# Turning the first chunk of two passes earlier, halving the last chunk, and moving a branch, in a four-layer graph kernel

## The reference, cut to what matters

```python
x = _layernorm(x + _L0_gnn_ref(x, adj, L0_gnn_embedding, L0_gnn_weight, L0_gnn_bias))
x = _layernorm(x + _L1_gnn_ref(x, 0, L1_gnn_net_params, adj))        # z = relu((adj @ z) @ w[i]), twice
x = _layernorm(x + _L2_gnn_ref(x, adj, w_self, w_neighbor, bias))    # x @ w_self + (adj @ x) @ w_neighbor + bias
x = _layernorm(x + _L3_gnn_ref(x, adj, adj, weight, bias))           # [x, A x, 2AAx-x, A x, 2AAx-x] @ weight + bias
```

## Time and profile before

| what | us |
|---|---|
| median of 3 runs | 1255.47 (1253.18 to 1255.48) |
| the profiled execution, whole | 1256.36 |
| its span, first to last instruction | 1254.4 |
| PE busy in the span | 1230.7 (98%) |
| DVE busy | 758.2 (60%) |
| ACT, POOL busy | 215.7, 62.7 |

### The profile page before, as it was taken

How to read it: one execution, slowest core, us unless ns; L and a number is a source line. 1 busy time by engine, 2 the same in 40 slices (tenths; PEclk the granted TensorE clock), 3 DMA queues, 4 the chain that set the end, 5 groups by cost and what they waited for, 6 DMA issues and landing times.

```text
span 1254.4 us, 16358 instructions
## 1 busy us (share of the span) xinstructions
PE 1230.7 (98%) x5872; PEld 1031.1 (82%) x5872; DVE 758.2 (60%) x1863; ACT 215.7 (17%) x392; POOL 62.7 (5%) x52
## 2 busy tenths in 40 slices
PE   8999999999999999999999999999999999999996
PEld 6888888888888887888888888878888888888875
DVE  5825898777777877788725554552246255545624
ACT  6622111120111101120111111110111111111110
POOL 0000000000000000000000001010000000010100
PEclk9999999999999999999999999999999999999998
DMA  9832112111111110101011133043011111320320
GB/s 343 328 101 60 32 45 76 56 57 38 58 55 55 47 38 28 40 22 42 15 34 35 32 79 71 5 118 67 1 37 31 35 34 30 85 65 7 95 58 36
DMA packets 128646, 78.16 MB, mean 62 GB/s; under 512 B 97312, under 2 KB 108064, under 8 KB 126752
## 3 DMA queue, kind: packets, MB, share of 16 engines
q1 hardware_dynamic: 128560, 77.05, 21.2%
HBM read 53.42 MB, written 23.59 MB: 61 GB/s over the span
## 4 chain that ended last, share of the span: by engine, by line
PE 93%; DVE 3%; DMA 2%; SPq 1%; issue 1%; ACT 0%; DVEq 0%
PE ps L679 29%; PE ps L680 29%; PE ps L783 22%; PE ps L697 8%; PE ps L718 2%; PE ps L719 2%; DMA raw<-in_at 1%; PE ps L691 1%; DVE nat L1045 1%; DVE ring L1045 1%; DMA td<-ring 0%; DMA ring<-td 0%; SPq L1087 0%; DVE ring L931 0%; DVE sml L987 0%
## 5 line engine op out<-in xcount | busy, mean ns | idle before, releaser
L679 PE MATMUL ps<-B,xs 128*128 128x512 f32 x1664 | 655.0, 394 | 1.5 <-DVE xs L943 1.5
L680 PE MATMUL ps<-B,xs 128*128 128x512 f32 x1664 | 648.2, 390 | 0.0
L679 PEld LDWEIGHTS ps<-B,xs 128*128 128x128 f32 x1664 | 312.9, 188 | 64.2 <-issue 1.6
L680 PEld LDWEIGHTS ps<-B,xs 128*128 128x128 f32 x1664 | 312.9, 188 | 62.5
L783 PE MATMUL ps<-Tw,xs 128*128 128x512 f32 x1280 | 309.4, 391 | 0.9 <-DVE ring L1045 0.9
L783 PEld LDWEIGHTS ps<-Tw,xs 128*128 128x128 f32 x1280 | 238.4, 188 | 53.3 <-DVE ring L1045 4.2
L931 DVE TENSOR_TENSOR ring<-ps,rrep 128x512 f32<-128x512 f32 x94 | 64.5, 689 | 259.1 <-PE ps L680 247.5
L1045 DVE SCALAR_TENSOR_TENSOR nat<-ps,embn,nat 128x128 f32<-128x128 f32 x448 | 153.3, 342 | 51.5 <-PE ps L783 51.3
L1045 DVE SCALAR_TENSOR_TENSOR ring<-ps,embn,ring 128x128 f32<-128x128 f32 x512 | 174.8, 341 | 0.0
L697 PEld LDWEIGHTS ps<-W,ring 128*128 128x128 f32 x896 | 112.7, 193 | 10.7 <-issue 3.1
L697 PE MATMUL ps<-W,ring 128*128 128x128 f32 x896 | 114.3, 277 | 3.4 <-DMA ring<-td 2.3
(11 more groups left out here) (66 smaller groups left out, 569.2 us busy)
## 6 DMA issues: line engine op xcount, KB each, us to landing
raw<-in_at SPq DMA_DIRECT2D x13, 1024.0 KB, 16.9
td<-ring SPq DMA_DIRECT2D x32, 256.0 KB, 2.1
ring<-td SPq DMA_DIRECT2D x128, 64.0 KB, 2.5
ring<-in_xn SPq DMA_DIRECT2D x16, 256.0 KB, 2.9
ring_x<-in_xt SPq DMA_DIRECT2D x32, 128.0 KB, 3.2
ring_x<-y1d SPq DMA_DIRECT2D x32, 128.0 KB, 3.2
out<-nat SPq DMA_DIRECT2D x16, 256.0 KB, 2.3
y1d<-ring SPq DMA_DIRECT2D x14, 256.0 KB, 2.8
```

The costliest lines, as they stand in the source:

```text
L679: pe.matmul(bank, x[:, 0, m, :], of, start=m == 0, stop=False)
L680: mm = pe.matmul(bank, x[:, 1, m, :], of, start=False, stop=ends and m == NT - 1)
```

## The change

It has three parts.

1. The step `turn` of the first chunk of passes 4 and 5 stands where the lane's previous pass ends (behind its last `normed`), ahead of the first of the two hand-overs, and its `back` stands behind that hand-over. Both stood at the first chunk's own product. The second chunk's `turn` and `back` move up by two quarters of the first chunk's product.
2. In the very last pass (pair 1, pass 6) the last chunk of 512 columns is done as two of 256, numbered 4 and 5, with a hand-written order. The last multiplication of `normed` for chunks 1 and 2 of that pass goes from DVE to POOL (`pooled`), and chunks are written out as they become ready. Chunk 5's `centre` waits for POOL's `normed` of chunk 1, whose small buffer it reuses.
3. DVE, ACT, POOL and SP read the flag behind the step `scale` of chunk 1 of that pass (`CUT`), a chunk and a half before the end. The general body stands in the branch that is taken if the flag is set, and the remaining steps of the fast one behind it, in the `Else`. PE still reads the flag at its end.

The diff, cut to its core:

```diff
-            if p == 6 and j != 1:
+            if p == 6:
                 put("out", j, 6, c)
+        if (j, p) == (1, 6):
+            order = order[:12]
         for c, m in order:
-            if p in (4, 5) and (c, m) == (0, 0):
-                turn(0, 0)
-            if p in (4, 5) and (c, m) == (0, 1):
-                put("back", j, p, 0, 0)
-            if p in (4, 5) and c < 3 and m == 2:
+            if p in (4, 5) and c < 3 and m == (2 if c else 0):
                 turn(c + 1, 0)
-            if p in (4, 5) and c < 3 and m == 3:
+            if p in (4, 5) and c < 3 and m == (3 if c else 1):
                 put("back", j, p, c + 1, 0)
...
+        if (j, p) == (1, 6):
+            for m in range(4):
+                put("mm", j, p, 4, m)
+                if m == 1:
+                    put("after", j, p, 2)
+                    put("deviate", j, p, 1)
+                    put("centre", j, p, 2)
+            put("scale", j, p, 4)
+            put("normed", j, p, 1)
+            exchange(1)
+            put("mm", j, p, 5, 0)
+            put("mm", j, p, 5, 1)
+            put("deviate", j, p, 2)
+            put("normed", j, p, 2)
+            exchange(2)
+            put("after", j, p, 4)
+            put("centre", j, p, 4)
+            put("mm", j, p, 5, 2)
+            put("mm", j, p, 5, 3)
+            put("scale", j, p, 5)
+            put("deviate", j, p, 4)
+            put("after", j, p, 5)
+            put("centre", j, p, 5)
+            put("normed", j, p, 4)
+            exchange(4)
+            put("deviate", j, p, 5)
+            put("normed", j, p, 5)
+            exchange(5)
+            return
...
         for p in (4, 5, 6):
+            if p < 6:
+                put("turn", j, p, 0, 0)
             yield
+            if p < 6:
+                put("back", j, p, 0, 0)
...
-END = STEPS.index(Step("out", 1, 6))
+CUT = STEPS.index(Step("scale", 1, 6, 1)) + 1
+
+def pooled(s):
+    return (s.j, s.p) == (1, 6) and s.c in (1, 2)
...
+                        if c == 4:
+                            dv.wait_ge(s_norm, norm_at[Step("normed", j, p, 0)])
+                        if c == 5:
+                            dv.wait_ge(s_pn, pool_at[Step("normed", j, p, 1)])
...
+                    if s.kind == "normed" and pooled(s):
+                        po.wait_ge(s_rec, rec_at[s])
+                        po.tensor_tensor(g, g, sml[:, n, c, 0, :].unsqueeze(2).to_broadcast([P, 8, C]),
+                                         ALU.mult).then_inc(s_pn, 1)
...
-                fast.dve(eng, STEPS)
+                fast.dve(eng, STEPS[:CUT])
                 eng.wait_ge(s_flag, 1)
                 v = eng.value_load(flag[0:1, 0:1], min_val=0, max_val=N)
                 with eng.If(v != 0):
...
                     slow.dve(eng, STEPS)
+                with eng.Else():
+                    fast.dve(eng, STEPS[CUT:])
...
-                fast.sp(eng, STEPS[:END])
+                fast.sp(eng, STEPS[:CUT])
...
-                with eng.If(v == 0):
-                    fast.sp(eng, STEPS[END:])
-                with eng.Else():
+                with eng.If(v != 0):
                     fast.sp_start(eng)
                     slow.sp_start(eng)
                     slow.sp(eng, STEPS)
+                with eng.Else():
+                    fast.sp(eng, STEPS[CUT:])
```

More of the change, by code:

```diff
@@ L23 @@
 LAST = 15
+SPAN = [(512 * c, 512) for c in range(NC)] + [(1536, 256), (1792, 256)]
 PIECES = {0: 4, 1: 2, LAST: 4}
@@ L275, in second @@
                     yield
-        if j == 1:
-            for c in range(NC):
-                put("out", j, 6, c)
     def whole_pair(j):
@@ L470, in way @@
             prep2_at = {s: 2 * v for s, v in numbered("prep2").items()}
-            mean_at, var_at, norm_at = numbered("centre"), numbered("deviate"), numbered("normed")
+            mean_at, var_at, rec_at = numbered("centre"), numbered("deviate"), numbered("normed")
+            norm_at = {s: i + 1 for i, s in enumerate(s for s in rec_at if not pooled(s))}
+            pool_at = {s: i + 1 for i, s in enumerate(s for s in rec_at if pooled(s))}
             n_T = len(T_at)
@@ L581, in way @@
                         sq_after[s] = held_q[n]
-                        held_q[n] = (s_var, var_at[Step("deviate", s.j, s.p, s.c)])
+                        if s.c != 4:
+                            held_q[n] = (s_var, var_at[Step("deviate", s.j, s.p, s.c)])
             def tile_landed(m, c):
@@ L591, in piece, with span, within @@
                 return slice(c * width, (c + 1) * width)
+            def span(c):
+                return slice(SPAN[c][0], sum(SPAN[c]))
+            def within(slot, c):
+                return slot[:, 256 * (c - 4):256 * (c - 3)] if c > 3 else slot
             def ch(t, c):
-                return t[:, c * 512:(c + 1) * 512]
+                return t[:, span(c)]
             def groups(t, c):
@@ L618, in y_slot @@
                             ring[:, 4, :], ring[:, 5, :], ring_x[:, 0, :], ring_x[:, 1, :]][4 * j + c]
-                return ring[:, 4 + j % 2, :]
+                return within(ring[:, 4 + j % 2, :], c)
             def square_slot(j, p, c):
@@ L625, in square_slot @@
                     return rrep[:, 1536:2048] if general else ring_g[:]
-                return ps[:, 6 + j % 2, :]
+                return within(ps[:, 6 + j % 2, :], c)
             def part_slot(c):
@@ L677, in pe_quarter @@
                 for m in range(4 * k, 4 * k + 4):
-                    of = B[:, m, c * 512:(c + 1) * 512]
+                    of = B[:, m, span(c)]
                     pe.matmul(bank, x[:, 0, m, :], of, start=m == 0, stop=False)
@@ L681, in pe_quarter, with pe_rest @@
                 return mm
-            def pe_rest(pe, x, bank, v):
+            def pe_rest(pe, x, bank, c, v):
                 for m in range(NT):
                     pe.wait_ge(s_glo, 16 * (v - 1) + m + 1)
-                    pe.matmul(bank, x[:, 0, m, :], glo[:], start=False, stop=m == NT - 1).then_inc(s_gmm, 1)
+                    pe.matmul(bank, x[:, 0, m, :], glo[:, 0:SPAN[c][1]], start=False, stop=m == NT - 1).then_inc(s_gmm, 1)
             def pe_turned(pe, bank, src):
@@ L692, in pe_turned, with pe_weighed @@
                 return mm
-            def pe_weighed(pe, bank, *pairs):
-                for k in range(4):
+            def pe_weighed(pe, bank, c, *pairs):
+                for k in range(SPAN[c][1] // P):
                     for i, (src, w) in enumerate(pairs):
@@ L957, in dve_steps @@
                         dv.wait_ge(s_four, four_at[s])
-                        bank = ps[:, nbank_of[s, "four"], :]
+                        bank = ps[:, nbank_of[s, "four"], 0:SPAN[c][1]]
                         if p == 3:
@@ L968, in dve_steps @@
                             if p == 6:
-                                dv.wait_ge(s_v, v_at[after(j, 5, c)])
+                                dv.wait_ge(s_v, v_at[after(j, 5, min(c, 3))])
                             else:
@@ L1126, in sp_steps @@
                     j, p, c, k, n = s.j, s.p, s.c, s.k, s.j % 2
-                    cols = slice(c * 512, (c + 1) * 512)
+                    cols = span(c)
                     if s == STEPS[0] and not general:
@@ L1248, in _ @@
                 with eng.If(v != 0):
+                    fast.dve(eng, [s for s in STEPS[CUT:] if s.kind in ("scale", "after")])
                     eng.memset(bad[:], 0.0).then_inc(s_here, 1)
```

48 lines of the change are left out of this document (29 added, 19 removed).

## The result

The changed kernel takes **1247.17 us** (median of 5 runs, 1246.30 to 1247.71); the kernel before, run beside it, 1253.18 (1252.71 to 1255.48). The ratio is 0.994, 95% interval 0.9927 to 0.9954: faster, by 6.0 us. In a second set of runs it took 1247.90 against 1255.05, ratio 0.994 (0.9926 to 0.9953), 7.15 less. The forecast was 1246.7.

The account below looks back on a forecast made before the run. PE is busy nearly throughout, so only its stalls, clock falls and the stretch behind its last product can pay. 1255.47 - (4.2 - 0.1 + 1.8 + 0.2 + 2.7 = 8.8) = 1246.7 us, range 1244.0 to 1250.0.

Parts of the forecast that it names:

- The lower bound (only the waits): Earlier turns in passes 4 and 5: gain 2.5 us if only PE's waits go and no clock loss, against 4.2 forecast.
- The cost of the earlier turns: Moved transposes, write and reads: 0.05 us charged twice on DVE, otherwise nothing; POOL's bias stays at its place in the order.
- the case that the prediction said no row shows: POOL and DVE instructions with two SBUF inputs meeting, DVE second: blocked until POOL's ends, by the skill's rule; 0.3 us priced.
- Rival 4: Last chunk's 256-column fp32r matmuls lose the 512-column rate, 0.447 us each: slower kernel, 1268 us; chance 0.04.
- The meeting of POOL and DVE: Last pass's tail: DVE's subtraction of `centre` 4 comes while POOL multiplies, costing 0.3 us, bounds 0 and 1.3.
- the cover of 1.0: Behind `scale` of chunk 1, last pass: 0.1 plus 0.9 us spare hides DVE's jump; beyond 1.0 each microsecond counts fully.
- Rival 1: DVE's mid-pass jump is not hidden, taking 6.5 to 7.5 us instead of 4.4: about 1248.5 us; chance 0.14.
- Rivals 2 to 4: Respectively: end still jumps, 1249.4 us (chance 0.07); PE waits there for another transfer, 1250.8 (0.03); narrow matmuls slow, 1268 (0.04).
- 0.2 off for the last `out`: Kernel's end: the last store, half as long, saves 0.2 us of the 2.6 behind DVE's end, bounds 0 and 1.
- PE's jump is covered: Kernel's end: PE's jump of 3.6 us ends at 1247.6, before SP's wait ends at about 1249.3, so costs nothing.
- The base: Starting time of the kernel before from which the gains were subtracted: 1255.47 us, the median of its runs.
- the 8.8 forecast: Total gain over the kernel in us: 4.2 - 0.1 + 1.8 + 0.2 + 2.7, giving 1246.7.

Follow-up runs that it names:

- part 1 alone: Kernel before, with only the first chunks of passes 4 and 5 turned at the end of the lane's previous pass: 1250.66 us, ratio 0.9968.
- the longer wait: Changed kernel with one first chunk (fourth lane, pass 5) turned late and its four reads held until DVE's second turn behind it: 1251.57 us, ratio 0.9984.
- the later cut: Changed kernel with the outcome read one chunk later, behind `scale` of chunk 2 of the last pass: 1247.09 us, ratio 0.9947.
- PE's later read: Changed kernel in which PE waits for DVE's last `after` before reading the outcome: 1246.08 us, ratio 0.9927.
- part 3 alone: Kernel before, with the outcome read by every engine behind `scale` of chunk 1 of the last pass, last chunk whole: 1252.62 us, ratio 0.9976.

## Why the prediction was right, and where it was off

**Part 1: right in size and mechanism.** The forecast was 4.1; part 1 alone gave 4.25 by the medians, and the profiles of before and after differ by 4.34 there. The reading of the earlier trace rows, that 3.7 are lost where the wait is 2.0, is borne out by the longer wait: what exceeded it was the clock again, 1.7. The lower bound (only the waits) was needed: with PE standing 1.9 the clock once stayed up.

**The cost of the earlier turns: nothing, as forecast, but one effect was not seen.** POOL's bias was said to stay at its old place. In order it does; in time it follows the turn and now meets DVE's splits, which have two inputs in SBUF. Groups on the profile's page of after, for the earlier trace rows:

```profile
L1129 POOL TENSOR_TENSOR nat<-nat,bias 128x512 f32<-128x512 f32 x32 | 43.0, 1344 | 542.2 <-DVE ring L1003 246.8
...
L991 DVE TENSOR_TENSOR xs<-nat,xs 128x512 fp32r<-128x512 f32 x72 | 54.9, 805 | 12.8 <-ACT xs L863 12.4
```

The bias took 1295 ns in before, the 72 splits 682 each (46.0 us in all), so the splits keep DVE busy 8.9 us longer. Part 1 alone has the same (806). The means hide what happens: in the trace of after 64 splits take what they took, and eight, one for each first chunk that is turned early, take 1766 to 1795 ns, 1.1 us more. One of them, and the bias that it meets (DVE's and POOL's timelines):

```profile
815.66 1.78 DVE L991 TENSOR_TENSOR xs<-nat,xs 128x512 fp32r<-128x512 f32 x1
```

```profile
815.39 1.50 POOL L1129 TENSOR_TENSOR nat<-nat,bias 128x512 f32<-128x512 f32 x1 [36.67 <-ACT xs L863]
```

DVE's split begins 0.27 behind POOL's start and ends 0.54 behind POOL's end, where a whole one takes 0.68: it was held for most of POOL's time. This is the case that the prediction said no row shows, DVE as the second of the two. PE's wait for the splits is 1.5 as before, so the cover was there; nothing in the forecast had measured it.

**Part 2: 1.8 forecast at DVE's end, 1.93 measured.** The matmul was put at 0.115 and took 0.120. Rival 4 was answered with "at any width"; the records show products in f32 twice at 64 and 128 columns, and in fp32r once at 512 and, in after, at 256 (64 records for 64 matmuls). No other width occurs here. POOL's multiplication was put at 1.3 and took 1.04. The meeting of POOL and DVE was put at 0.3, on the subtraction; it cost 0.19, on the small operation in front of it (0.36 for 0.17), which ended at 1235.59 as POOL's multiplication did (1235.56; POOL's timeline of after):

```profile
1234.52 1.04 POOL L1121 TENSOR_TENSOR nat<-nat,sml 128x512 f32<-128x512 f32 x1 [0.44 <-DVE sml L1042]
```

The Trainium skill (SBUF — State Buffer, "Who interferes with whom") names `tensor_scalar` among the operations of DVE that can take the ports shared with POOL, and says that the later one waits for all of the earlier one; this row agrees, and without POOL's multiplication it took 0.17. The subtraction began behind POOL's end, so it was not held here.

**Part 3: 2.7 forecast, 2.7 to 2.8 measured alone,** of which 2.4 to 2.6 are SP's jump and 0.25 the last store, which the forecast didn't have. DVE was to go on 4.4 behind the start of the `scale` and did so at 4.0; the cover of 1.0 held, with 0.5 of idle to spare in front of the next `scale`. Rival 1 didn't come about, and the later cut shows what it would have cost, 1.1. Rivals 2 to 4 are out by the rows above: 0.2 behind SP's wait, no turned block in PE's waits, 0.120 a matmul.

**The step that failed: 0.2 off for the last `out`, because it is half as long, and with it that PE's jump is covered.** The jump was taken for covered because it ends before SP's wait does. It does so (1240.8 against 1244.0), but it isn't the last of it: another 16 KB are fetched behind it, beside the last store, and the store was 0.7 to 1.1 longer than before where 0.2 less was forecast. Without that it would have been 0.7 shorter. From DVE's end to the span's end 2.9 were forecast and 3.8 and 4.2 came; with PE's later read it was 2.4. The Trainium skill (Runtime: NRT & Kernel Launch, "Instruction fetch mechanics") says that code comes in blocks of 16 KiB through a DMA queue of the engine's own, at a cost mostly hidden; the trace agrees on the size for the fetches on q8 (16,384 bytes; those on q14 are 8,192). On the cost it does not: here the store landed 1.4 and 1.8 us later with the fetch beside it (3.3 and 3.7) than without (1.9).

**The base.** The forecast went from 1255.47, the median of three runs. Beside the later kernels the kernel before had medians of 1253.18 to 1255.05, so some of the 2.8 us between the 8.8 forecast and the 6.0 first measured is the base. The profiles, without their first stretch, differ by 8.1. That the forecast time of 1246.7 lies within 0.5 of the first median is thus partly luck: the base was 0.4 to 2.3 too high, and the gain came out 1.65 to 2.8 smaller than forecast.

## What to carry to other kernels

A branch at the end of an engine's program is not over when the engine has taken it: look at what it fetches, and at which transfer is under way on the DMA engines then. Moving an engine's last read later, behind a wait that costs it nothing, can be worth as much as a shorter chain of work (1.8 us here for one wait, 1.93 for the halves). A stall of PE is to be priced together with the stretch behind it, since the clock can nearly double its cost, or not, at nearly the same length. And a group's mean can hide a few long instructions: look at the single ones.

## What the runs showed of the hardware that was not expected

- A fetch of 16,384 bytes of instructions took 0.9 to 1.7 us on one DMA engine and held that engine's share of the last store, of 128 KB: its 16th landing came 1.2 to 1.9 us behind the others, in six profiles of six in which the fetch began 0.82 to 0.99 us behind the store's issue, and at most 0.1 behind them in the four in which it began 1.19 or more behind it.
- The last store, of 128 KB, landed in 1.9 us where it was not held; one of 256 KB in 2.3 with no fetch beside it (part 3 alone), and in 2.6 with one of 8,192 bytes (before).
- PE's jump over the general body took 3.3 to 3.75 us in 14 profiles, DVE's 3.9 and 4.0 from the start of the operation in front of it to the next one, SP's 2.7 to 2.8 from its last wait to its drain.
- DVE's operation on 4 columns per partition was held by a POOL operation, 0.36 for 0.17; eight of DVE's 72 splits took 1.77 to 1.80 us for 0.68 because they began behind POOL's start, with no effect on the end.
- PE's granted clock fell to half behind an idle time of 1.89 us in one profile and stayed full behind one of 2.17 at the same place in another.
